# A decoder layer for four batches on one core: activation tables loaded in other places, expert weights ahead of their second biases, and no filler matmuls in the first batch

## The reference

```python
x = x + softmax_causal(ln(x) Wq (ln(x) Wk)^T / sqrt(128)) (ln(x) Wv)         # one head
x = x + cross_attention(ln(x), context, mask)                                 # 16 heads of 8
h = ln(x)
a = rope_self_attention(h)                                                    # 16 heads of 8
x1 = ln(h + a) * g1 + be1
gate = softmax(x1 @ Wg + bg); two best of 8 experts, weights renormalised
y_e = gelu(x1 @ W1[e] + b1[e]) @ W2[e] + b2[e]                                # 512 hidden
x = x + ln(x1 + sum over the two of weight * y_e) * g2 + be2
```

## Time and profile before

| | us |
|---|---|
| median of 3 runs | 685.74 (682.94 to 687.50) |
| the profiled execution | 684.35 |
| its span, first to last instruction | 682.56 |
| PE busy | 608.9 (89%) |
| DVE busy | 453.7 (66%) |
| ACT busy | 345.6 (51%) |
| POOL busy | 121.5 (18%) |

### The profile page before, as it was taken

How to read it: one execution, slowest core, us unless ns; L and a number is a source line. 1 busy time by engine, 2 the same in 40 slices (tenths; PEclk the granted TensorE clock), 3 DMA queues, 4 the chain that set the end, 5 groups by cost and what they waited for, 6 DMA issues and landing times.

```text
span 682.6 us, 11214 instructions
## 1 busy us (share of the span) xinstructions
PE 608.9 (89%) x4086; PEld 386.0 (57%) x4086; DVE 453.7 (66%) x1126; ACT 345.6 (51%) x618; POOL 121.5 (18%) x121
## 2 busy tenths in 40 slices
PE   6899899999998999999998989999999999886960
PEld 3664454437645764468836754478647644376950
DVE  4673588937854779657836778677726689479224
ACT  0405126874144458866254568755435488552530
POOL 5100100001041200001053400031136100220433
PEclk8999999999999999999999999999999999988985
DMA  6300000001025460003146640012155610126861
GB/s 205 124 0 1 1 0 2 1 1 39 1 92 162 138 181 2 1 1 110 29 123 174 186 121 1 1 39 64 36 171 153 203 54 2 31 79 192 281 177 42
DMA packets 45085, 54.98 MB, mean 81 GB/s; under 512 B 4346, under 2 KB 35432, under 8 KB 45032
## 3 DMA queue, kind: packets, MB, share of 16 engines
q1 hardware_dynamic: 43240, 50.61, 25.4%
q0 software_dynamic: 1792, 3.67, 1.8%
HBM read 46.73 MB, written 7.54 MB: 80 GB/s over the span
## 4 chain that ended last, share of the span: by engine, by line
PE 61%; DVE 20%; ACT 6%; issue 5%; POOL 3%; SPq 2%; DMA 1%; POOLq 0%; DVEq 0%; ACTq 0%
PE banks L1810 8%; PE banks L1796 5%; PE banks L1455 5%; PE banks L1441 5%; PE banks L1777 4%; DVE nm L1263 3%; PE banks L1759 3%; PE banks L1660 3%; PE banks L1692 2%; PE banks L1690 2%; ACT px L900 2%; PE banks L1663 2%; POOL rstd L615 2%; DVE hat L947 2%; PE banks L1709 2%
## 5 line engine op out<-in xcount | busy, mean ns | idle before, releaser
L1263 DVE TENSOR_REDUCE nm<-banks 128x1 fp32r<-128x512 f32 x256 | 157.7, 681 | 23.9 <-PE banks L1777 23.4
L900 ACT ACTIVATE px<-banks 128x1024 f32<-128x1024 f32 x128 | 127.8, 1026 | 21.3 <-PE banks L1796 21.3
L723 ACT ACTIVATE hT<-banks,wp 128x128 f32<-128x128 f32 x216 | 61.6, 370 | 60.8 <-PE banks L1441 60.5
L615 POOL TENSOR_TENSOR rstd<-ve,misc 128x4 f32<-128x4 f32 x19 | 19.5, 1028 | 404.8 <-DVE ve L941 404.8
L1777 PE MATMUL banks<-kst,qst 32*128 32x512 f32 x256 | 81.8, 495 | 1.5 <-ACT kst L873 0.8
L1810 PE MATMUL banks<-px,vf 128*32 128x256 f32 (+1 forms) x832 | 76.7, 440 | 5.6 <-ACT ot L906 2.5
L1441 PE MATMUL banks<-xT,wp 128*128 128x128 f32 x432 | 59.8, 282 | 4.1 <-ACT hT L723 2.7
L1796 PE MATMUL banks<-q2st,kst 32*128 32x512 f32 x256 | 59.1, 495 | 2.8 <-ACT px L900 2.8
L1455 PE MATMUL banks<-wp,hT 128*128 128x128 f32 x432 | 59.3, 282 | 2.1 <-ACT hT L723 2.1
L1441 PEld LDWEIGHTS banks<-xT,wp 128*128 128x128 f32 x432 | 53.9, 194 | 10.8 <-issue 5.2
L1455 PEld LDWEIGHTS banks<-wp,hT 128*128 128x128 f32 x432 | 54.4, 197 | 3.5 <-ACT hT L723 2.7
(11 more groups left out here) (283 smaller groups left out, 1030.5 us busy)
## 6 DMA issues: line engine op xcount, KB each, us to landing
wp<-in_experts SPq DMA_DIRECT2D x54, 514.0 KB, 4.6
b2r<-in_L_ffn_b SPq DMA_DIRECT2D x53, 64.0 KB, 4.3
px<-in_experts SPq DMA_DIRECT2D x6, 514.0 KB, 6.1
expert_rows<-xs SPq DMA_DIRECT2D x12, 256.0 KB, 5.1
xs<-expert_tokens SPq DMA_DIRECT2D x9, 256.0 KB, 3.0
msk<-in_mask SPq DMA_DIRECT2D x4, 308.0 KB, 3.2
xin<-in_x SPq DMA_DIRECT2D x4, 256.0 KB, 2.9
ot<-in_const_sel SPq DMA_DIRECT2D x1, 1024.0 KB, 5.1
```

The costliest lines, as they stand in the source:

```text
L615: pool.tensor_tensor(rstd[:, n, :], ve[:, n, :], exponent, ALU.pow).then_inc(k[f"ln_rstd{n}"], 1)
L723: ins = act.activation(hT[:, n % 2, c * P:(c + 1) * P], bank[h_bank(p, i)][:, c * P:(c + 1) * P], ACT.Gelu, bias=weights(n, 2 * FF + c, 2 ...
L900: act.activation(px[:, c % 2, 2 * i:2 * i + 2, :], banks[:, 4 + 2 * i:6 + 2 * i, :], ACT.Exp, scale=SCALE_H).then_inc(k["f_exp"], 1)
L1263: dve.tensor_reduce(nm[:, t, g, BLK * hh:BLK * hh + 1], bank[s1_bank(g, t, i)], AX.X, ALU.max, negate=True).then_inc(k["f_max"], 1)
```

## The change

It does four things.

1. `load_table(func)` is a ScalarE activation of one column, so that the table is loaded there. It stands at the start of `opening` and of `cross` (Exp), behind cross attention's exponentials (Gelu), behind the gelus `o3` in `self_attention` (Exp), and in the last `tail` (Gelu).
2. In the last batch SyncE issues the weights of tiles 0 to 7 first, with the two stores of batch 2 between them, and the eight bias rows behind them all.
3. `experts(p, label)` for p < 0 does nothing: 86 fillers go, the 19 of the opening stay.
4. The order of TensorE is changed at three places: in the opening keys, queries and values come ahead of the biases' transpose; in `cross`, `down(p, 0)` ahead of the transposes `turn_rows(2, ...)`; in the first `tail` the gate's logits ahead of the query stacks.

```diff
-WARM = {"w3": 12, "w5a": 8, "w5b": 6}
...
                 e = sp.value_load(eid[0:1, p % 2, i:i + 1], min_val=0, max_val=NE - 1)
                 sp.dma_start(weights(n, 0, WP),
                              experts_in[bass.DynSlice(e, 1)].rearrange("e p c -> (e p) c")).then_inc(w_in[w_slot(n)], 16)
+                if n < NT * (B - 1) or i >= WSLOTS + WMORE:
+                    load_bias(p, i, e)
+
+            def load_bias(p, i, e):
                 g = NG * p + i // YG
                 if g >= 2 and b2_place(g) < 2:
                     sp.wait_ge(k["y_out"], g - 1)
...
                     for i in range(YG):
                         load_expert(B - 1, i)
                     keep_y(p, NG - 2)
+                    for i in range(YG, WSLOTS + 1):
+                        load_expert(B - 1, i)
                     keep_y(p, NG - 1)
-                    for i in range(YG, WSLOTS + WMORE):
+                    for i in range(WSLOTS + 1, WSLOTS + WMORE):
                         load_expert(B - 1, i)
+                    for i in range(WSLOTS + WMORE):
+                        load_bias(B - 1, i, sp.value_load(eid[0:1, (B - 1) % 2, i:i + 1], min_val=0, max_val=NE - 1))
...
+            def load_table(func):
+
+                i = next(table_columns)
+                act.activation(table_out[:, i:i + 1], euler[:, 0:1], func)
...
             def opening():
                 act.wait_ge(k["zeroed"], 11)
+                load_table(ACT.Exp)
                 context_copies(0, 7, 6)
...
                 for label in X_GAPS:
                     gelus(p - 1, label)
+                if n:
+                    load_table(ACT.Exp)
                 act.wait_ge(k["x_q2_mm"], G * n + 1)
...
+                if p >= 0:
+                    load_table(ACT.Gelu)
                 gelus(p, "w0")
...
                 gelus(b - 1, "o3")
+                if b:
+                    load_table(ACT.Exp)
                 copy_q2(0)
...
             def experts(p, label):
                 if p < 0:
-                    keep_warm(WARM.get(label, 4 * len(gap_tiles(label))), H_BANKS[0])
                     return
...
                     up(p, 0)
                     up(p, 1)
-                turn_rows(2, n, hat3, 0)
                 if p >= 0:
                     down(p, 0)
+                turn_rows(2, n, hat3, 0)
...
             def opening():
                 turn_rows(0, 0, hat1, 0)
+                front_keys_queries(0)
+                front_values(0)
                 pe.wait_ge(k["early_loaded"], 16 * N_EARLY_LOADS)
                 pe.transpose(bank[3][:, 0:NROWS], rows, eye[0:NROWS, 0:NROWS]).then_inc(k["rows_turned"], 1)
-                front_keys_queries(0)
+                pe.wait_ge(k["casts"], 3)
+                x_turn(0, 7, 6)
                 pe.wait_ge(k["bias_cols"], 1)
...
-                front_values(0)
-                pe.wait_ge(k["casts"], 3)
-                x_turn(0, 7, 6)
                 front_scores(0)
```

More of the change, by code:

```diff
@@ L15 @@
+import itertools
 from contextlib import ExitStack
@@ L371, in build @@
         slot = sb("slot", [P, 2, 2 * T], I32)
+        table_out = sb("table_out", [P, 3 * B + 1])
         xs = sb("xs", [P, NT, D])
@@ L713, in _ @@
         def _(act):
+            table_columns = itertools.count()
+            def load_table(func):
+                i = next(table_columns)
+                act.activation(table_out[:, i:i + 1], euler[:, 0:1], func)
             def gelus(p, label):
@@ L794, in tail @@
                     gelus(p - 1, "tb")
+                if not ahead:
+                    load_table(ACT.Gelu)
                 if after:
@@ L1306, in opening @@
                 mask_bias(0)
-                dve.wait_ge(k["rows_turned"], 1)
-                dve.tensor_copy(cols[:, 0:NROWS], bank[3][:, 0:NROWS]).then_inc(k["bias_cols"], 1)
                 dve.wait_ge(k["a_kq"], 1)
@@ L1314, in opening @@
                 dve.tensor_copy(va[:].rearrange("p t d -> p (t d)"), bank[0]).then_inc(k["a_v"], 1)
+                dve.wait_ge(k["rows_turned"], 1)
+                dve.tensor_copy(cols[:, 0:NROWS], bank[3][:, 0:NROWS]).then_inc(k["bias_cols"], 1)
                 dve.wait_ge(k["rot_cols"], 1)
@@ L1644, in tail @@
                     experts(p - 1, "tf")
+                if p == 0:
+                    gate_logits(p)
                 if ahead:
                     x_query_stacks(n)
-                if after:
+                if p > 0:
                     gate_logits(p)
```

## The result

The changed kernel took 693.79 us as the median of 7 runs (689.74 to 705.82), the kernel before 684.97 beside it (7 runs). The ratio is 1.0075, with an interval of 1.0048 to 1.0102. The forecast was 677.7 us, the range 671.5 to 683.5. The profiled execution has a span of 688.2 against 682.6 us and a mean granted clock of 0.945 against 0.975.

The account below looks back on a forecast made before the run. The chain that ended last was taken as PE 61%, DVE 20%, ACT 6%. The terms -2.5 - 1.5 - 1.1 + 2.0 - 1.5 - 1.0 - 2.4 sum to -8.0, giving 677.7 us, range 671.5 to 683.5.

Parts of the forecast that it names:

- The low clock: Batch 0 without fillers: two to four half-clock stretches of about 3.4 us expected, costing +2.0 us (0 to +6).
- fillers of self-attention: Batch 0's self-attention: fillers in four places make DVE's maxima wait for PE; removing them gains 1.1 us.
- The slower rival: Self-attention of batch 0: PE does not recover its clock between gaps, 15.3 us lost, 691.0 us in all; chance 0.06.
- Cross attention's fillers: Batch 0's cross attention: DVE's maxima wait for PE behind four fillers in three places; removing them gains 1.5 us.
- The opening: Start of the kernel: keys and queries start 1.6 us earlier, scores between 13.9 and 14.9; -2.5 us (-1.6 to -3.0).
- Tables: Three Exp loads ahead of self-attention's first exponentials, batches 1 to 3: 0.5 us each saved, -1.5 us (0 to -3.8).
- down(0): `down(0)` ahead of the transposes fills batch 1's idle stretch, so the clock stays full there; -1.0 us (-1.7 to 0).
- The last batch: Earlier weights remove PE's 4.65 us wait; last `up` at 653.5 in place of 655.88, -2.4 us (0 to -6.3).
- the first rival: Last batch: ninth tile's weights, issued behind the biases, make PE wait over 4 us; gain 0, 680.1 us; chance 0.18.

Follow-up runs that it names:

- a_fill_ln: The changed kernel with only the 26 fillers around batch 0's layer norm and rope put back; ratio 1.0109 to the kernel before.
- a_fill: The changed kernel with the removed fillers put back and every other edit kept; ratio 0.9981 to the kernel before.
- b_nox: The kernel before without the 12 fillers of batch 0's cross attention, all other fillers kept; ratio 0.9967.
- b_tables: The kernel before with only the table loads moved; ratio 0.9983.
- b_loads_again: Second run of b_loads, the kernel before with only the last batch's loads in the change's order; ratio 0.9956, with the stops.
- b_loads3: The kernel before with six last-batch weights first, each later weight followed by an earlier tile's bias; ratio 0.9905 with the stops, 0.9983 without.
- b_nofill: The kernel before with only the fillers removed; ratio 1.0126.
- a_fill_sa: The changed kernel with only the 16 fillers between self-attention's first scores put back; ratio 1.0086 to the kernel before.
- b_loads: The kernel before with only the last batch's loads in the change's order; ratios 0.9954 and 0.9956 with the stops, 1.0016 without.
- b_loads2: b_loads with the ninth tile's weights directly behind the eighth's and biases from kept registers; ratio 0.9937 to the kernel before, with the stops.
- b_open: The kernel before with only the opening's new order, the bias columns' copy behind those of keys, queries and values; ratio 1.0005.
- best: The changed kernel with fillers back except cross attention's 12, and b_loads3's load order; ratio to the kernel before 0.9852 with the stops, 0.9913 without.

## Why the prediction was wrong

- **The low clock, +2.0 (ends 0 and +6): this is the step that failed.** With the fillers of self-attention (-1.1) it came to +0.9; measured are +7.0 from cross attention's output to the next keys of batch 0. I counted stretches of 3.4 us and set each against a gap; the text said that in both low rows of the trace the clock came back with PE busy. Those rows were of projections and experts. In self-attention it did not come back so soon: 27.30 us in the change, 54.61 in a_fill_ln. With all fillers in place (a_fill) this part has no stretch at 0.50 and takes 67.0 us, as before. The slower rival named this place, and its mechanism is the one that happened; I gave it 0.06 on the strength of rows from other stages. Its price of 15.3 was for all of 82.45 to 108.
- By the Trainium skill's rule ("TensorE: Matmul & The Clock Gate", "Why this matters for your kernels") idle gaps put the clock back to half. The trace agrees that idle time stands ahead of each fall (PE busy 1.02 us of the 3.41 ahead of 80.27 and 1.39 ahead of 93.93 in the change, 2.08 in a_fill_ln); but the cost lay in how long the clock stayed low afterwards, and a_fill_ln shows that filling the first gap does not save it.
- **Cross attention's fillers, -1.5:** right; b_nox measured -1.68, and 1.8 between the same two instructions in the other profiles.
- **The opening, -2.5: wrong.** Keys 1.34 us earlier (1.6 predicted), the scores 0.42 later, the first maximum 0.39 later. From the values to the scores PE takes 4.39 us in place of 2.62: 1.1 more for the values and the context's transposes, whose records are longer, and 0.7 for the biases' transpose and product. I had put these beside DVE's copies; that held for the transpose, but both stand ahead of the scores on PE, and the product runs when the copies are done. The faster start that I counted on came in three of eight profiles with this order.
- **Tables, -1.5:** right in size and reason, 0.5 a batch. The Trainium skill ("ScalarE: Activation LUTs", "What ACT_TABLE_LOAD costs") has a drain beside each load; the estimate from its figures was -8.0. It did not show: the interval of b_tables ends at 0.9962, 2.7 us, and in the kernel before the load stands without a gap between the copy ahead of it and the exponential behind:

```profile
253.12 0.68 ACT L880 ACTIVATE kst<-banks,misc 128x512 fp32r<-128x512 f32 x1
253.82 1.28 ACT L900 ACT_TABLE_LOAD   x1
255.12 1.02 ACT L900 ACTIVATE px<-banks 128x1024 f32<-128x1024 f32 x1
```

- **down(0), -1.0: wrong.** The stretch at 222 us is missing in the change, but also in b_nox and b_loads_again, which have the old order. It stands in 4 of the 12 profiles with the old order and in none of the 8 with the new one, so the order may help, but no pair of runs shows it. Where it stands it costs 0.6 us from cross attention's output to the first second-scores (37.5 in place of 36.9), not the 1.7 that I priced it at. Without the early Gelu load the move is a loss.
- **The last batch, -2.4: wrong; the first rival (0.18) was right in place and size**, a wait of 6.08 us ahead of the ninth with the low clock behind it. I had written down its issue (about 636) and not asked when PE would want it: PE was free at 641.2 in the change, the weights were issued at 641.77 and landed 5.5 us later. On the old scale the last `up` came at 655.6, where I had 653.5 and the kernel before 655.88.

By the stages as measured the sum is -0.4 + 7.0 + 0.8 - 0.6 - 1.4 - 0.3 = +5.1 at the last down, where the table has +5.03; the span gave +5.6. The -0.4 is up to cross attention's output: +0.4 of the opening, -1.8 of its fillers, and +1.0 of the stretch near 32 us, which the profile of the kernel before happens not to have. The -0.6 is batch 1 from 222.84 to 259.74 (the stretch at 222 us, which that profile has), the -1.4 the tables, the -0.3 the last batch.

## What to carry to other kernels

A filler is priced by the stretch that it protects: ask not how long the clock falls in its gap, but whether the work behind the gap has ever brought the clock back in a trace. Remove fillers place by place: removing those of cross attention paid, removing all of them cost more than that, and those of the tail and of the next cross attention were never tried alone. A transfer moved forward on a queue moves something back: take for each tile behind it the time at which it is wanted, less its flight, and follow the queue to its last entry: b_loads3 gained 7.8 us on PE and kept about 1 at the end, and a store moved from in front of other stores gave about 3 more.

## What the runs showed of the hardware that was not expected

- **The clock can stay at half while PE is busy.** 53.83 of 54.61 us busy at 0.50 (a_fill_ln), and 13.65 of 13.65 (b_nofill). Of the 289 matmuls there, 254 have weights of 32*128 or 128*32; the fillers, with 128*128, were running as it came back in a_fill_sa. Whether it is the shape was not tried apart. In the change it came back at 121.23 with no filler at all.
- **The same place gives a low stretch in one profile and not in the next**, near 32 us (11 of 20 profiles, 1 us each) and near 222 us (4 of 20, 0.6 us) above all. Of one profile a difference of that size says nothing; the terms here were taken from pieces between such stretches.
- **Stops of all engines.** On two occasions (b_loads, b_loads2, b_tables, b_open; then b_loads3, b_loads_again, b_nox, best) each kernel had stops in batches 2 and 3 at the same work, and one more in the last batch, in which PE, DVE and ACT did nothing. The profile puts their end down to `remote`, not to an instruction of the kernel (ACT 5.91 us until 389.27 in b_open). In b_open, 386.30 to 389.20 us (columns as in the stretches above):

```profile
386.30:389.20 2.90, 0.00 (x0) 0.00 (x0) 0.00 (x0) 0.00 (x0) 1.33 (x2) 0.73 0.90 264
```

They come with busy DMA engines (0.90), but busy engines alone do not make them: the kernel before has 0.97 in the same 2.90 us, with PE busy throughout. One chip showed them on one occasion and not on the next. The clock fell behind them, and in three of the kernels (b_open, b_loads, b_tables) it then stayed at 0.50 for 17 us in self-attention of batch 2 or 3, where experts and not fillers stand between the scores. With them the kernels take some 18 us more. Their cause is open.
- **A bias issued by itself costs SP 1.1 us, one behind its weights 0.5** (eight in a row took 8.27 us from the first's start to the last's end, after; a pair's bias follows its weights by 0.5, before and after).
